# Self-attention of a three-part layer: normalisations moved to ScalarE, bias additions moved from TensorE to GpSimd

## The reference

```
x = x + attn(layernorm(x))                 # 16 heads of 16, sequences of 64
attn: q = rope(n @ Wq.T + bq); k = rope(n @ Wk.T + bk); v = n @ Wv.T + bv
      out = softmax(q k.T * scale) v;  return out @ Wo.T + bo
x = x + ffn(layernorm(x))                  # gates = sigmoid(layernorm(x) @ Wg), top 2 of 8 experts
```

## Time and profile before

| | |
|---|---|
| median of 3 runs (lowest, highest) | 2087.81 us (2086.94, 2091.26) |
| the profiled execution | 2089.35 us, span of its instructions 2087.6 us |
| busy in the span | PE 98%, DVE 72%, ACT 59%, POOL 48% |
| self-attention stage | about 1315 to 1570 us of the span |
| inside it, 1358 to 1530 us, busy of 172.0 us | PE 171.6, DVE 160.9, POOL 148.5, ACT 131.8 |
| a step in the loop | 7.26 us |

### The profile page before, as it was taken

How to read it: one execution, slowest core, us unless ns; L and a number is a source line. 1 busy time by engine, 2 the same in 40 slices (tenths; PEclk the granted TensorE clock), 3 DMA queues, 4 the chain that set the end, 5 groups by cost and what they waited for, 6 DMA issues and landing times.

```text
span 2087.6 us, 48252 instructions
## 1 busy us (share of the span) xinstructions
PE 2036.8 (98%) x16424; PEld 1800.0 (86%) x16425; DVE 1500.3 (72%) x2690; ACT 1235.6 (59%) x3015; POOL 995.5 (48%) x821
## 2 busy tenths in 40 slices
PE   8999999999999999999999999899998999999997
PEld 7889998998988898899899988688877888888886
DVE  7676766767767767767767666799986877666665
ACT  5665666656656665656656665477773435555553
POOL 6433334333333433333333343488882435777775
PEclk9999999999999999999999999999999999999999
DMA  4001001000000000010010001255532222333332
GB/s 159 16 16 36 17 18 35 15 20 25 25 20 25 15 30 25 10 35 20 15 35 15 20 11 45 76 164 167 163 104 89 91 71 49 54 55 53 53 55 41
DMA packets 99645, 103.89 MB, mean 50 GB/s; under 512 B 10912, under 2 KB 89120, under 8 KB 99584
## 3 DMA queue, kind: packets, MB, share of 16 engines
q1 hardware_dynamic: 85952, 84.47, 13.0%
q0 software_dynamic: 13632, 18.62, 5.5%
HBM read 72.52 MB, written 30.54 MB: 49 GB/s over the span
## 4 chain that ended last, share of the span: by engine, by line
PE 74%; POOL 9%; issue 6%; DVE 5%; ACT 2%; DMA 2%; POOLq 0%; SPq 0%; DVEq 0%; ACTq 0%
PE banks L997 42%; PE banks L1103 5%; PE banks L1088 5%; PE banks L1052 5%; POOL out_dram L2534 4%; PE banks L1775 4%; POOL r_x L2498 3%; PE banks L2373 2%; POOL index L2505 2%; DMA out_dram<-r_y,index 2%; PE banks L1034 1%; PE banks L1797 1%; PE banks L1838 1%; PE banks L1854 1%; PE banks L2393 1%
## 5 line engine op out<-in xcount | busy, mean ns | idle before, releaser
L476 POOL TENSOR_TENSOR rinv<-rsum,inverse 128x4 f32<-128x4 f32 x112 | 112.8, 1007 | 480.0 <-ACT probs L612 480.0
L997 PE MATMUL banks<-ctxT_hi,qk_hi 128*128 128x256 f32 x1024 | 300.1, 293 | 0.0
L997 PE MATMUL banks<-ctxT_hi,qk_lo 128*128 128x256 f32 x1024 | 288.6, 282 | 0.0
L997 PE MATMUL banks<-ctxT_lo,qk_hi 128*128 128x256 f32 x1024 | 287.7, 281 | 0.0
L619 ACT ACTIVATE pc<-banks 128x512 f32<-128x512 f32 x256 | 155.8, 610 | 222.2 <-PE banks L997 222.2
L612 ACT ACTIVATE probs<-banks,nbias 128x256 f32<-128x256 f32 x512 | 236.4, 487 | 85.5 <-DVE nbias L760 85.5
L709 DVE TENSOR_TENSOR pT_lo<-banks,pT_hi 128x512 fp32r<-128x512 f32 x256 | 164.9, 686 | 112.6 <-ACT pT_hi L562 111.7
L755 DVE TENSOR_REDUCE peak<-banks 128x4 f32<-128x1024 f32 x128 | 156.6, 1224 | 120.0 <-PE banks L997 120.0
L479 POOL TENSOR_TENSOR probs<-probs,rinv 128x1024 f32<-128x1024 f32 x112 | 212.1, 1894 | 20.3 <-POOL rinv L476 20.3
L997 PE MATMUL banks<-pT_hi,ctx_hi 128*128 128x512 f32 x512 | 207.1, 405 | 3.6 <-DVE pT_lo L709 1.7
L997 PE MATMUL banks<-pT_hi,ctx_lo 128*128 128x512 f32 x512 | 201.9, 394 | 0.0
(11 more groups left out here) (282 smaller groups left out, 6098.0 us busy)
## 6 DMA issues: line engine op xcount, KB each, us to landing
ctx_raw<-in_ctx_dram SPq DMA_DIRECT2D x64, 256.0 KB, 2.7
experts_w<-in_L_ffn_We_dram SPq DMA_DIRECT2D x24, 512.0 KB, 3.9
x_in<-in_x_dram SPq DMA_DIRECT2D x16, 256.0 KB, 2.8
x_again<-in_x_dram SPq DMA_DIRECT2D x16, 256.0 KB, 2.8
x_stream<-z SPq DMA_DIRECT2D x16, 256.0 KB, 2.2
s_x<-x_stream SPq DMA_DIRECT2D x32, 128.0 KB, 3.7
s_x_again<-x_stream SPq DMA_DIRECT2D x32, 128.0 KB, 3.1
x_normalised<-s_xl SPq DMA_DIRECT2D x32, 128.0 KB, 1.7
```

The costliest lines, as they stand in the source:

```text
L476: nc.gpsimd.tensor_tensor(rinv[:, s % 2, :], rsum[:, s % 2, :], inverse[:, :], ALU.pow).then_inc(rinv_done, 1)
L997: last = nc.tensor.matmul(out, a, b, start=(n == 0), stop=(n == 3 * len(pairs) - 1))
```

## The change

The bias products on TensorE and the matrices they need go. For queries and keys the rotated biases `turned_bias` are computed once by VectorE, and GpSimd adds them to `spun` in each step, after the sum of the two rotation products (a new semaphore `turn_added` stands between). The output bias is added by GpSimd to `x1_again` one step ahead of its use, after the load has landed. Both normalisations become ScalarE copies with a scale and a bias, and GpSimd computes their `shift` after each `rstd`.

```diff
     def inverse_spread(pool, g, s):
...
             pool.wait_ge(rstd_done, g.tile(s, 4))
-            pool.sem_inc(pool_past, 1)
+            pool.sem_inc(past, 1)
+        if first:
+            nc.gpsimd.tensor_scalar(shift[:, 0:1], mv[:, 0, 0:1], rstd[:, 0:1], -1.0, ALU.mult, ALU.mult).then_inc(mean_done, 1)
+        if second:
+            nc.gpsimd.tensor_scalar(shift[:, 1:2], mv[:, 1, 0:1], rstd[:, 1:2], -1.0, ALU.mult, ALU.mult).then_inc(shift_done, 1)
...
     def pool_step_at(pool, g, s):
         inverse_spread(pool, g, s)
-        if g.has(s, 3):
-            if g.has(s, 2):
-
-                wait_filled(pool, g, ("xT", s))
+        if g.has(s, 2):
+
+            wait_freed(pool, g, ("qk", s))
+            pool.sem_inc(past, 1)
+            nc.gpsimd.tensor_tensor(turned, turned, spun[:, 1, :], ALU.add).then_inc(turn_added, 1)
+        if g.has(s, -1):
             o = (s + 1) % 2
-            pool.sem_inc(pool_past, 1)
-            normalised(xn[:, :], x1[:, o, :], 0).then_inc(ln_done, 1)
+            pool.wait_ge(x1_reloaded[o], 16 * (g.at + s))
+            nc.gpsimd.tensor_tensor(x1_again[:, o, :], x1_again[:, o, :], biases[:, 2 * D:], ALU.add).then_inc(x1_biased, 1)
         if g.has(s, 2):
-
-            wait_freed(pool, g, ("qk", s))
-            nc.gpsimd.tensor_tensor(turned, turned, spun[:, 1, :], ALU.add).then_inc(turn_done, 1)
-        if g.has(s, -2):
-            if g.has(s, -4):
-
-                pool.wait_ge(xl_stored[s], 16 * g.at)
-                key, pairs_on = before(g, s, ("x3T", s))
-                wait_filled(pool, g, key, pairs_on)
-            pool.sem_inc(pool_past, 1)
-            normalised(xl[:, s, :], x2[:, s, :], 1).then_inc(l3_done, 1)
+            if not g.has(s, 1):
+                pool.wait_ge(bias_done, 1)
+            pool.wait_ge(turn_added, g.tile(s, 3))
+            nc.gpsimd.tensor_tensor(turned, turned, turned_bias[:, :], ALU.add).then_inc(turn_done, 1)
...
     def act_step(act, g, s):
...
+        if g.has(s, 3):
+            act.wait_ge(mean_done, g.tile(s, 4))
...
+                wait_filled(act, g, ("xT", s))
+            copy(xn[:, :], x1[:, o, :], scale=rstd[:, 0:1], bias=shift[:, 0:1]).then_inc(ln_done, 1)
+        if g.has(s, -1):
             bank, free = wait_filled(act, g, ("o", s))
...
             copy(out, bank[:, 0:8]).then_inc(free, 1)
+
+        if g.has(s, -2):
+            act.wait_ge(shift_done, g.tile(s, -1))
...
+            copy(xl[:, s, :], x2[:, s, :], scale=rstd[:, 1:2], bias=shift[:, 1:2]).then_inc(l3_done, 1)
...
     def dve_start(dve):
...
-        step(nc.vector.tensor_tensor(bias_lo[:, :], biases[:, :], bias[:, :], ALU.subtract))
-        link(nc.vector.tensor_scalar(bias_even[:, :], bias[:, :].bitcast(F32), table[:, 2 * HD:2 * HD + 1], None, ALU.mult))
-        nc.vector.scalar_tensor_tensor(out=bias[:, :], in0=bias_lo[:, :], scalar=table[:, 2 * HD + 1:2 * HD + 2],
-                                       in1=bias_even[:, :], op0=ALU.mult, op1=ALU.add).then_inc(bias_done, 1)
+        step(rotate(biases[:, 0:2 * D], 0))
+        link(rotate(biases[:, 0:2 * D], 1))
+        nc.vector.tensor_tensor(turned_bias[:, :], turned, spun[:, 1, :], ALU.add).then_inc(bias_done, 1)
...
     def dve_step_at(dve, g, s):
...
-            dve.wait_ge(x1_reloaded[s], 16 * g.at)
+            dve.wait_ge(x1_biased, g.tile(s, -1))
...
     def pe_step(pe, g, s):
...
-            nc.tensor.matmul(bank[:, 0:D], share_r[:, :], bias[:, 2 * D:], start=True, stop=False)
             for m in range(DC):
-                last = nc.tensor.matmul(bank[:, 0:D], oT[:, m, :], woT[:, m, :], start=False, stop=(m == DC - 1))
+                last = nc.tensor.matmul(bank[:, 0:D], oT[:, m, :], woT[:, m, :], start=(m == 0), stop=(m == DC - 1))
...
-            nc.tensor.matmul(bank, share_r[:, :], bias[:, 0:2 * D], start=True, stop=False)
             exact3(bank, [((xT_hi[:, s, c, :], xT_lo[:, s, c, :]),
-                           (w_hi[:, c, 0:2 * D], w_lo[:, c, 0:2 * D])) for c in range(DC)], True).then_inc(done, 1)
+                           (w_hi[:, c, 0:2 * D], w_lo[:, c, 0:2 * D])) for c in range(DC)]).then_inc(done, 1)
```

More of the change, by code:

```diff
@@ L1331, in self_attention @@
     probs = sb("probs", [P, 2, 1024])
-    setup = Region(nc, early.at, 6 * 1024)
-    bias_lo = sb("bias_lo", [P, 3 * D], F32, setup)
-    bias_even = sb("bias_even", [P, 3 * D], F32, setup)
     pT = sb("pT", [P, DC, 512])
@@ L1342, in self_attention @@
     biases = sb("biases", [P, 3 * D])
-    bias = sb("bias", [P, 3 * D], F32R)
-    share = sb("share", [P, P])
-    share_r = sb("share_r", [P, P], F32R)
     bvp = sb("bvp", [P, DC])
@@ L1353, in self_attention @@
     rstd = sb("rstd", [P, 2])
+    shift = sb("shift", [P, 2])
+    turned_bias = sb("turned_bias", [P, 2 * D])
     xT_hi = sb("xT_hi", [P, 2, DC, P], F32R)
@@ L1370, in self_attention @@
     pool_setup = sem("pool_setup")
-    pool_past = sem("pool_past")
-    bias_hi = sem("bias_hi")
+    past = sem("past")
+    mean_done = sem("mean_done")
+    turn_added = sem("turn_added")
     bias_done = sem("bias_done")
@@ L1395, in self_attention @@
     dve_step = sem("dve_step")
-    pool_step = sem("pool_step")
-    dve_past = sem("dve_past")
+    shift_done = sem("shift_done")
+    x1_biased = sem("x1_biased")
     bank_turns = [Turns(lambda kind, k=k: [key for key in pair_order(kind) if bank_of(key) == k],
@@ L1516, in pool_start @@
         nc.gpsimd.memset(power[:, :], -0.5).then_inc(pool_setup, 1)
-        nc.gpsimd.memset(share[:, :], 2.0 / P).then_inc(pool_setup, 1)
         nc.gpsimd.memset(vbd[:, :, :, :, :, :], 0.0).then_inc(pool_setup, 1)
-        pool.wait_ge(pool_setup, 3)
+        pool.wait_ge(pool_setup, 2)
     def inverse_spread(pool, g, s):
@@ L1535, in pool_step_at @@
         inverse_spread(pool, g, s)
-        if g.has(s, 3):
-            if g.has(s, 2):
-                wait_filled(pool, g, ("xT", s))
-            o = (s + 1) % 2
-            pool.sem_inc(pool_past, 1)
-            normalised(xn[:, :], x1[:, o, :], 0).then_inc(ln_done, 1)
         if g.has(s, 2):
             wait_freed(pool, g, ("qk", s))
-            nc.gpsimd.tensor_tensor(turned, turned, spun[:, 1, :], ALU.add).then_inc(turn_done, 1)
-        if g.has(s, -2):
-            if g.has(s, -4):
-                pool.wait_ge(xl_stored[s], 16 * g.at)
-                key, pairs_on = before(g, s, ("x3T", s))
-                wait_filled(pool, g, key, pairs_on)
-            pool.sem_inc(pool_past, 1)
-            normalised(xl[:, s, :], x2[:, s, :], 1).then_inc(l3_done, 1)
+            pool.sem_inc(past, 1)
+            nc.gpsimd.tensor_tensor(turned, turned, spun[:, 1, :], ALU.add).then_inc(turn_added, 1)
+        if g.has(s, -1):
+            o = (s + 1) % 2
+            pool.wait_ge(x1_reloaded[o], 16 * (g.at + s))
[5 more added lines that the diff above has]
+            nc.gpsimd.tensor_tensor(turned, turned, turned_bias[:, :], ALU.add).then_inc(turn_done, 1)
         if g.has(s, 0):
@@ L1571, in act_start @@
         act.wait_ge(small_in, 16 * 6)
-        act.wait_ge(pool_setup, 3)
+        act.wait_ge(pool_setup, 2)
         for j in range(4):
@@ L1577, in act_start @@
             nc.scalar.activation(out, src, ACT.Identity).then_inc(setup_hi, 1)
-        nc.scalar.activation(bias[:, :], biases[:, :], ACT.Identity).then_inc(bias_hi, 1)
-        nc.scalar.activation(share_r[:, :], share[:, :], ACT.Identity).then_inc(bias_hi, 1)
     def copy(out, src, **kw):
@@ L1628, in act_step @@
             copy(out, bank[:, 0:8]).then_inc(free, 1)
+        if g.has(s, -2):
+            act.wait_ge(shift_done, g.tile(s, -1))
+            if g.has(s, -4):
+                act.wait_ge(xl_stored[s], 16 * g.at)
+                key, pairs_on = before(g, s, ("x3T", s))
+                wait_filled(act, g, key, pairs_on)
+            copy(xl[:, s, :], x2[:, s, :], scale=rstd[:, 1:2], bias=shift[:, 1:2]).then_inc(l3_done, 1)
     def scalar(act):
@@ L1659, in dve_start @@
         dve.wait_ge(small_in, 16 * 6)
-        dve.wait_ge(bias_hi, 1)
-        step(nc.vector.tensor_tensor(bias_lo[:, :], biases[:, :], bias[:, :], ALU.subtract))
-        link(nc.vector.tensor_scalar(bias_even[:, :], bias[:, :].bitcast(F32), table[:, 2 * HD:2 * HD + 1], None, ALU.mult))
-        nc.vector.scalar_tensor_tensor(out=bias[:, :], in0=bias_lo[:, :], scalar=table[:, 2 * HD + 1:2 * HD + 2],
-                                       in1=bias_even[:, :], op0=ALU.mult, op1=ALU.add).then_inc(bias_done, 1)
+        step(rotate(biases[:, 0:2 * D], 0))
+        link(rotate(biases[:, 0:2 * D], 1))
+        nc.vector.tensor_tensor(turned_bias[:, :], turned, spun[:, 1, :], ALU.add).then_inc(bias_done, 1)
         dve.wait_ge(bias_done, 1)
@@ L1672, in mean_of @@
         dve.wait_ge(dve_step, stats_at)
-        dve.sem_inc(dve_past, 1)
+        dve.sem_inc(past, 1)
         step(nc.vector.bn_aggr(mv[:, which, :], stats[:, which, :]))
@@ L1762, in pe_start @@
         pe.wait_ge(weights_in, 16 * 4)
```

(4 more changed lines are left out.)

## The result

The changed kernel takes 2093.06 us (median of 12 executions, 2091.04 to 2096.89), the kernel before 2087.8 us (12 executions beside it). The ratio is 1.0023, 95% interval [1.0016, 1.0031]: slower by 0.23%. The forecast was 2085.7 us with a range up to 2091.5. A second measurement of the two gave 1.0023 again, [1.0013, 1.0032].

The account below looks back on a forecast made before the run. TensorE looked like the bound of self-attention steps, with VectorE and a loop of waits through GpSimd close behind. Profiled 2089.35 + 0.0 (loop) - 2.1 (ends) = 2087.2 us; against the median 2085.7, range 2080.5 to 2091.5.

Parts of the forecast that it names:

- The loop: Waits through VectorE, GpSimd and TensorE in self-attention, closing over two steps: 14.55 us, 7.27 a step, no change in time.
- the link: From VectorE's `mv` through GpSimd's operations to TensorE's transposes of `spun`: lengthened from 3.68 to 4.80 us.
- The new wait: TensorE ahead of its transposes of `spun`, released by GpSimd's add of the biases: 0.2 to 0.4 us in each step.
- ScalarE: Two added activations, about 0.56 us each, fit its waits ahead of `oT` and `xT_hi`: cost 0, at most 0.1 us.
- VectorE's floor: Shortest self-attention step VectorE allows, about 7.10 us, capping TensorE's gain at 0.16 us a step.
- The ends: First tiles and last steps of the self-attention stage: together 2.1 us faster.
- the first two openings: Bias products that TensorE opens after waits at the first and second tile: removing them saves 0.54 and 0.32 us.
- the run-out: Last steps of self-attention: 0.44 us saved on output bias products, 0.33 us on GpSimd's work ahead of a late product.
- The rival on the other side: GpSimd's operations lengthen the link by 0.63 us, a step by 0.31: slower, 2093.2 us, chance 0.17.

Follow-up runs that it names:

- before_no_products: Kernel before without the two bias products on TensorE, all three biases left out of the computation: 2083.86 us, ratio 0.998.
- no_qk_add: Changed kernel without GpSimd's add of the rotated biases, so queries and keys get no bias: 2085.7 us, ratio 0.9985 to the kernel before.
- after_fill: Changed kernel with 16 identity transposes filling each of TensorE's two long waits of turn 0: 2091.61 us, ratio 1.0017 to the kernel before.
- x1_last_fill: x1_add_last with TensorE's two long waits of turn 0 filled with identity transposes: 2086.57 us, ratio 0.9993 to the kernel before.
- x1_add_last: Changed kernel with GpSimd's add to `x1_again` moved behind its add of the rotated biases: 2089.88 us, ratio 1.0004 to the kernel before.
- qk_bias_on_pe: Changed kernel with the biases of queries and keys back on TensorE, the other two parts kept: 2088.75 us, ratio 1.0002 to the kernel before.

## Why the prediction was wrong

- **The loop: right, its single terms in part by luck.** The forecast summed the link to 4.80 us, the loop over two steps to 14.55 and a step to 7.27; measured 4.83, 14.61 and 7.31. In the link two errors nearly cancel: the two shifts hold GpSimd 0.51 us (forecast 0.34), and the first of them starts 0.99 us after `mv` and not 1.17. The add to `x1_again` takes 0.74 us (forecast 0.73). The new wait has its place and its releaser; it is 0.50 us in every second step, where the forecast had 0.2 to 0.4 in each. From the seventh to the last transpose of `xn` the change cost 0.6 us, where the forecast had nothing.
- **ScalarE: right.** The activations take 0.60 and 0.61 us, inside my ends. The estimate from the page "ScalarE: Activation LUTs" of the Trainium skill (section "What ACT_TABLE_LOAD costs") was 0.59, and the trace agrees. The waits ahead of `oT` and `xT_hi` absorbed them: both are gone from the list of the stretch.
- **VectorE's floor: mis-sized.** 7.17 us and not 7.10. I had taken all of its wait for `xT_hi` as removable, 0.16 us a step; in before_no_products that wait is gone and the step is only 0.09 us shorter. It changes nothing in the verdict, since the link lies above both.
- **The ends: this is the step that failed.** The forecast gave -2.1 us, summed from the openings of the bias products, and said that at the third tile "the link of GpSimd takes it back". Measured on the profiles: from the first to the seventh transpose of `xn` +2.95 us (+3.40 in the second pair), from the last one to the first product of the expert stage +0.2 in both. Three errors lie in it. In the steps where the pipeline fills, nothing covers the link, and the 1.4 us by which the add of the biases lengthens it come out as wait in full, twice: I had weighed the link for the loop, where it has slack, and then used only the removed products at the start. The run no_qk_add puts 2.3 us on these waits. Then I took the speed of TensorE behind a wait as given; the clock fell, and after_fill puts 2.2 us on that. Last, the 0.54 and 0.32 us credited to the first two openings were not seen: from the first to the third transpose of `xn` it was 14.16 and 14.14 us before and is 14.40 and 14.41. This stretch varies from profile to profile (12.90 us in x1_last_fill, 14.40 in x1_add_last, whose instructions are the same up to there), and why the credit was not seen stays open. At the other end, the 0.77 us credited to the run-out were taken back by the link as well: without the add (no_qk_add) or with the add to `x1_again` behind it (x1_add_last) the way from the last transpose of `xn` to the expert stage is 0.5 and 0.4 us shorter than before, not 0.2 longer.
- **The rival on the other side** had the right sign and place (a longer link) but for the wrong reason: it wanted 0.63 us more in every step of the loop. It was given from 4.98 us of link; at 4.83 the loop lost almost nothing and the kernel was slower all the same.
- **Left open.** From the first transpose of `xn` to the first expert product the change cost 3.8 us between the first two profiles and 4.2 between the second ones; the medians differ by 5.3 and 4.1 us. The profiles differ in two more places, where the runs change little. The time to the first transpose of `xn` runs from 1313.6 to 1317.5 us over the thirteen profiles. The first 30 us of the expert stage (from its first product to VectorE's fifth `f_h_lo`) take 30.1 us before, 30.8 in both profiles of the changed kernel and 27.7 to 32.6 over all. In them the granted clock is low for a longer or a shorter time; this is one stretch of the changed kernel, then the same of after_fill, where the 30 us were 31.7:

```profile
1575.00:1580.00 5.00, 3.69 (x17) 2.34 (x15) 1.23 (x1) 1.13 (x2) 2.81 (x9) 0.84 0.16 54
```

```profile
1575.00:1580.00 5.00, 4.47 (x14) 3.31 (x14) 0.00 (x0) 0.86 (x3) 0.29 (x3) 0.50 0.09 26
```

  So after_fill gave back 0.9 us behind the stage of the 2.2 it had gained at the start, in its one profile. With the 0.7 us at the experts the pairs of profiles come to 4.4 and 4.9 us, inside the intervals of the ratio. What decides how long the clock stays low there, and whether that is the part of qk_bias_on_pe's gain that its timings lack (its 30 us are 0.7 longer than before), was not settled.

## What to carry to other kernels

Work that moves off a full engine onto one that is half idle can still stand in the link between two others. Before counting the saving, add up the loop of waits, over two steps if it closes over two. An order that puts the awaited instruction first was worth 0.14 us a step here with no work removed. Weigh the same link in the steps where the pipeline fills, where it is paid in full. If TensorE is what waits there, price the work behind the wait at the lower clock too.

## What the runs showed of the hardware that was not expected

Waits of 2.4 and 2.0 us on TensorE, in a stretch where it was already loosely filled, brought its granted clock to 0.53 over 5 us, and products of 512 columns then took 0.63 us and not 0.39. Sixteen transposes of the identity, 1.9 us of otherwise useless work in each wait, gave back 2.2 us of the start in the profile. On GpSimd a 128x1 multiplication with two factors takes 0.27 us and holds the engine 0.23 to 0.28 us, a third of the 0.74 us of a 128x256 add that has 256 times the elements. In this kernel two such small operations are not free in a chain of waits: they took 0.51 us of the link.
